# A kernel with three stages on one core: the keys and queries of its random-feature attention split into a high and a low part, copied over all 128 rows by DMA, and multiplied by the feature projection in single-pass products

## The reference

```
x2 = layer_norm(x)                             # twice in a row, merged in the kernel
q, k, v = x2 @ wq + bq, x2 @ wk + bk, x2 @ wv + bv      # 16 heads of width 8
p(t)  = (t @ proj_mat) / sqrt(8)               # "angles": 8 x 128 projection, per token and head
phi(t) = concat(cos(p), sin(p)) / sqrt(128)
kv   = sum over tokens of phi(k)^T v           # per sequence of 256 tokens and head
attn = phi(q) @ kv
y = attn @ wo + bo + residual; y = y + relu(layer_norm(y) @ w1 + b1) @ w2 + b2
```

## Time and profile before

| what | value |
|---|---|
| median of 3 runs | 4777.37 us (4777.08 to 4777.64) |
| the profiled execution, its own time | 4773.44 us |
| span of the profiled execution | 4771.7 us |
| features phase | 0 to about 553 us |
| layers phase | about 554 to 4126 us |
| experts phase | about 4127 us to the end |

### The profile page before, as it was taken

One profiled execution on the slowest core, in us unless ns is written; L12 is line 12 of the kernel. 1 busy time (PEld: TensorE's weight loads), 2 busy tenths in 40 slices (PEclk: granted clock), 3 DMA queues, 4 the chain that ended last, 5 costly groups with the idle time before them and its releaser, 6 DMA issues. The chain is left out here.

```text
span 4771.7 us, 118293 instructions
## 1 busy us (share of the span) xinstructions
PE 4446.4 (93%) x45408; PEld 3473.7 (73%) x45408; DVE 3624.8 (76%) x6437; ACT 3026.3 (63%) x4718; POOL 1787.2 (37%) x966
## 2 busy tenths in 40 slices
PE   6999589999999999999999999999999999689999
PEld 2333278887788877888778887888878888468878
DVE  6888578888788888888878888788888878466553
ACT  5777367676667766776667676766766776233333
POOL 0000155554555545555445554555545555000000
PEclk9999799999999999999999999999999999889999
DMA  0000122222222222222222222222222222100000
GB/s 28 5 5 5 47 62 57 59 56 50 81 58 52 60 65 64 56 60 56 68 61 59 53 59 70 64 53 59 60 70 57 58 60 54 59 7 5 9 7 5
DMA packets 132797, 229.65 MB, mean 48 GB/s; under 512 B 29080, under 2 KB 33824, under 8 KB 131104
## 3 DMA queue, kind: packets, MB, share of 16 engines
q1 hardware_dynamic: 132256, 222.28, 17.9%
HBM read 29.23 MB, written 4.19 MB: 7 GB/s over the span
## 5 line engine op out<-in xcount | busy, mean ns | idle before, releaser
L660 POOL TENSOR_TENSOR qk_rotated<-qk_rotated,rotary_sines 128x1024 f32<-128x1024 f32 x384 | 922.9, 2403 | 1693.3 <-DVE rotary_sines L748 1693.3
L671 POOL TENSOR_TENSOR qk_rotated<-qk_rotated,rnorm 128x1024 f32<-128x1024 f32 x384 | 732.8, 1909 | 7.4
L756 DVE TENSOR_REDUCE qk_sumsq<-qk_squared 128x16 f32<-128x1024 f32 x384 | 467.5, 1218 | 297.6 <-ACT qk_squared L502 297.6
L221 PE MATMUL ps_proj<-qkv_w_hi,x_shifted_hi 128*128 128x512 f32 x1152 | 495.2, 430 | 36.5 <-DVE qkv_w_lo L716 24.0
L509 ACT ACTIVATE q_t<-ps_qk_t 128x512 f32<-128x512 f32 x384 | 229.4, 597 | 464.2 <-PE ps_qk_t L277 464.2
L738 DVE TENSOR_TENSOR qk_rotated<-ps_proj,rotary_scaled 128x1024 f32<-128x1024 f32 x384 | 467.9, 1219 | 7.6 <-ACT qk_squared L502 4.3
L748 DVE TENSOR_TENSOR rotary_sines<-ps_proj,rotary_scaled 128x1024 f32<-128x1024 f32 x384 | 467.0, 1216 | 1.6 <-POOL qk_rotated L660 1.6
L523 ACT ACTIVATE k_t_by_head<-ps_qk_t 64x512 f32<-64x512 f32 x768 | 452.0, 588 | 11.9 <-PE ps_qk_t L286 2.4
L223 PE MATMUL ps_proj<-qkv_w_hi,x_shifted_lo 128*128 128x512 f32 x1152 | 459.1, 399 | 0.0
L222 PE MATMUL ps_proj<-qkv_w_lo,x_shifted_hi 128*128 128x512 f32 x1152 | 458.1, 398 | 0.0
L502 ACT ACTIVATE qk_squared<-ps_proj 128x1024 f32<-128x1024 f32 x384 | 392.2, 1021 | 68.4 <-DVE qk_sumsq L756 50.1
(11 more groups left out here) (248 smaller groups left out, 9723.5 us busy)
## 6 DMA issues: line engine op xcount, KB each, us to landing
v_by_window<-v_tokens SPq DMA_DIRECT2D x1152, 128.0 KB, 2.4
v_by_window<-v_tokens SPq DMA_DIRECT2D x384, 64.0 KB, 2.1
v_by_window<-v_by_window SPq DMA_DIRECT2D x192, 64.0 KB, 2.0
qkv_w_raw<-in_layer_qk_dram SPq DMA_DIRECT2D x7, 1664.0 KB, 7.9
layer_w<-in_layer_w_dram SPq DMA_DIRECT2D x6, 580.5 KB, 3.9
layer_w<-in_layer_w_dram SPq DMA_DIRECT2D x6, 512.0 KB, 3.6
f_x<-in_x_dram SPq DMA_DIRECT2D x8, 256.0 KB, 5.7
x_attn<-f_y SPq DMA_DIRECT2D x8, 256.0 KB, 2.0
```

The lines of the kernel that those rows point to most:

```text
L221: mm(out, hi, HI[:, o:o + 512], start=True, stop=False)
L660: tt(u, u, TB[:], ALU.add).then_inc(added, 1)
L671: tt(u, u, r.unsqueeze(3).broadcast_to((P, 2, 8, DH)), ALU.mult).then_inc(scaled, 1)
L756: nc.vector.reduce_sum(SS[:, 16 * i:16 * i + 16], SQ[:].rearrange("p (h e) -> p h e", e=DH), AX).then_inc(sumsq, 1)
```

## The change

The keys and queries are no longer kept as one float32 tile of which 32 rows are multiplied. ACT writes them, with the bias, into a tile of the single-pass type float32r (the high part: k_hi, q_hi), and a new DVE instruction (k_low at step 11, q_low at step 12) computes PSUM plus bias minus the high part into a low part (k_lo, q_lo). SP then builds, for each of the four groups g of 32 rows, a stacked tile of 128 rows: high, low, high, low. That is 16 DMAs of 32 rows x 512 float32 (64 KB) for the keys and 16 for the queries of each block, SBUF to SBUF. At the start the projection is laid out to match: rows 0 to 63 hold it rounded to float32r, rows 64 to 127 what the rounding left. One float32r product over 128 rows thus sums the four partial products.

Further: project_q moves from step 11 to 12 and project_v from step 13 to 14 on PE, v_out from 13 to 14 on DVE; project_q now waits for the key's high and low part and project_v for the query's, since they overwrite the PSUM bank that those read. The key and query tiles have one buffer each in place of two. k_out waits until the stacked copies of the block before have landed. The store of a block's result is issued two blocks later in SP's list, behind the stacks. The input loads of blocks 1 to 7 share one semaphore.

```diff
-        PB, PBF = sb("proj_blocks", [P, BLK]), sb("proj_scaled", [P, BLK])
+        PB, PST = sb("proj_blocks", [P, BLK]), sb("proj_stacked", [P, BLK], F32R)
...
-        QT, KT = ([sb(f"{x}_t{k}", [P, BLK]) for k in range(2)] for x in ("q", "k"))
+        QHI, QLO, KHI, KLO = (sb(x, [P, BLK], F32R) for x in ("q_hi", "q_lo", "k_hi", "k_lo"))
+        QST, KST = sb("q_stacked", [P, 4, BLK], F32R), sb("k_stacked", [P, 4, BLK], F32R)
...
+        STACK = 16 * 16
...
+            def stack(dst, hi, lo, landed):
+                for g in range(4):
+                    rows = slice(32 * g, 32 * g + 32)
+                    for copy in range(2):
+                        sp.dma_start(dst[64 * copy:64 * copy + 32, g, :].bitcast(F32), hi[rows, :].bitcast(F32)).then_inc(landed, 16)
+                        sp.dma_start(dst[64 * copy + 32:64 * copy + 64, g, :].bitcast(F32), lo[rows, :].bitcast(F32)).then_inc(landed, 16)
+            def stack_k(b):
+                sp.wait_ge(k_hi, b + 1)
+                sp.wait_ge(k_lo, b + 1)
+                if b > 0:
+                    sp.wait_ge(angle, PAIRS * (b - 1) + 8)
+                stack(KST, KHI, KLO, k_in)
+            def stack_q(b):
+                sp.wait_ge(q_hi, b + 1)
+                sp.wait_ge(q_lo, b + 1)
+                after(sp, angle, PAIRS * b)
+                stack(QST, QHI, QLO, q_in)
...
             for i in range(NBLK):
-                sp.wait_ge(xo, 2 * i + 2)
-                sp.dma_start(x_attn[:, i, :], Y[i % 2][:]).then_inc(x_out[i % 2], 16)
+                stack_k(i)
+                stack_q(i)
+                if i > 1:
+                    store(i - 2)
+            store(NBLK - 2)
+            store(NBLK - 1)
...
             def project_q(b):
-                pe.wait_ge(proj_out, 2 * b + 1)
+                pe.wait_ge(k_hi, b + 1)
+                pe.wait_ge(k_lo, b + 1)
...
                 if u == 0:
-                    pe.wait_ge(proj_out, 2 * i + 1)
+                    pe.wait_ge(k_in, STACK * (i + 1))
                 if u == 8:
-                    pe.wait_ge(proj_out, 2 * i + 2)
+                    pe.wait_ge(q_in, STACK * (i + 1))
...
-                        last = mm(out, KT[i % 2][rows, c * P:(c + 1) * P], PBF[rows, :], start=True, stop=True)
+                        last = mm(out, KST[:, r, c * P:(c + 1) * P], PST[:], start=True, stop=True)
...
-                        last = mm(out, PBF[rows, j * P:(j + 1) * P], QT[i % 2][rows, :], start=True, stop=True)
+                        last = mm(out, PST[:, j * P:(j + 1) * P], QST[:, r, :], start=True, stop=True)
...
-                        if u == 11:
+                        if u == 12:
                             project_q(i + 1)
-                        if u == 13:
+                        if u == 14:
                             project_v(i + 1)
...
             def k_out(b):
                 act.wait_ge(proj, 3 * b + 1)
-                a(KT[b % 2][:], NB[:], ACT.Identity, bias=vec(AV_BK)).then_inc(proj_out, 1)
+                after(act, k_in, STACK * b)
+                a(KHI[:], NB[:], ACT.Identity, bias=vec(AV_BK)).then_inc(k_hi, 1)
...
-            ts(PBF[:], PB[:], float(1.0 / (np.sqrt(RD) * 2 * np.pi)), None, ALU.mult).then_inc(setup, 1)
+            ts(PB[:], PB[:], float(1.0 / (np.sqrt(RD) * 2 * np.pi)), None, ALU.mult).then_inc(setup, 1)
+            dve.wait_ge(setup, 4)
+            cp(PST[:], PB[:]).then_inc(setup, 1)
+            dve.wait_ge(setup, 5)
+            tt(PST[64:P, :], PB[64:P, :], PST[64:P, :].bitcast(F32), ALU.subtract).then_inc(setup, 1)
...
+            def k_low(b):
+                dve.wait_ge(k_hi, b + 1)
+                after(dve, k_in, STACK * b)
+                stt(KLO[:], NB[:], vec(AV_BK), KHI[:].bitcast(F32), ALU.add, ALU.subtract).then_inc(k_lo, 1)
...
+                        if u == 11:
+                            k_low(i + 1)
+                        if u == 12:
+                            q_low(i + 1)
-                        if u == 13:
+                        if u == 14:
                             v_out(i + 1)
```

More of the change, by code:

```diff
@@ L963, in features_phase @@
         KV, AB, G, NB = ps("kv"), ps("attn"), ps("tail"), ps("norm")
-        c_in, x_in, x_out, setup = sem("c_in"), [sem(f"x_in{k}") for k in range(NBLK)], [sem(f"x_out{k}") for k in range(2)], sem("setup")
+        c_in, x_in, x_out, setup = sem("c_in"), [sem(f"x_in{k}") for k in range(2)], [sem(f"x_out{k}") for k in range(2)], sem("setup")
         n_mean, n_cent, n_sq, n_var, n_arg, n_bc, n_out, n_aff = (sem("norm_" + x) for x in ("mean", "cent", "sq", "var", "arg", "bc", "out", "aff"))
@@ L968, in features_phase @@
         chain, rn, diag = sem("rs_chain"), sem("rnorm"), sem("diag")
-        proj, proj_out, vpad = sem("proj"), sem("proj_out"), sem("vpad")
+        proj, vpad = sem("proj"), sem("vpad")
+        k_hi, k_lo, q_hi, q_lo, k_in, q_in = (sem(x) for x in ("k_hi", "k_lo", "q_hi", "q_lo", "k_in", "q_in"))
         angle, rounded_act, rounded_dve, frac, fabs, feats, used = (sem(x) for x in ("angle", "rounded_act", "rounded_dve", "frac", "fabs", "feats", "used"))
@@ L973, in features_phase @@
         block = ctx.enter_context(nc.Block())
-        NSETUP = 7
+        NSETUP = 9
+        STACK = 16 * 16
         def vec(k):
@@ L994, in _, with store @@
             for i in range(1, NBLK):
-                sp.dma_start(X[:, i, :], xT[:, i, :]).then_inc(x_in[i], 16)
-            for i in range(NBLK):
-                sp.wait_ge(xo, 2 * i + 2)
-                sp.dma_start(x_attn[:, i, :], Y[i % 2][:]).then_inc(x_out[i % 2], 16)
+                sp.dma_start(X[:, i, :], xT[:, i, :]).then_inc(x_in[1], 16)
+            def stack(dst, hi, lo, landed):
[15 more added lines that the diff above has]
+                stack(QST, QHI, QLO, q_in)
+            def store(q):
+                sp.wait_ge(xo, 2 * q + 2)
+                sp.dma_start(x_attn[:, q, :], Y[q % 2][:]).then_inc(x_out[q % 2], 16)
+            for i in range(NBLK):
+                stack_k(i)
[4 more added lines that the diff above has]
+            store(NBLK - 1)
             for k in range(2):
@@ L1006, in norm_mean @@
             def norm_mean(b):
-                pe.wait_ge(x_in[b], 16)
+                pe.wait_ge(x_in[0], 16) if b == 0 else pe.wait_ge(x_in[1], 16 * (NBLK - 1))
                 if b > 0:
@@ L1050, in angles @@
                 if u == 0:
-                    pe.wait_ge(proj_out, 2 * i + 1)
+                    pe.wait_ge(k_in, STACK * (i + 1))
                 if u == 8:
-                    pe.wait_ge(proj_out, 2 * i + 2)
+                    pe.wait_ge(q_in, STACK * (i + 1))
                 for x in range(2):
                     r = 2 * (u % 2) + x
-                    rows, out = slice(32 * r, 32 * r + 32), TB[U % 2][:, x * BLK:(x + 1) * BLK]
+                    out = TB[U % 2][:, x * BLK:(x + 1) * BLK]
                     if u < 8:
                         c = u // 2
-                        last = mm(out, KT[i % 2][rows, c * P:(c + 1) * P], PBF[rows, :], start=True, stop=True)
+                        last = mm(out, KST[:, r, c * P:(c + 1) * P], PST[:], start=True, stop=True)
                     else:
                         j = u // 2 - 4
-                        last = mm(out, PBF[rows, j * P:(j + 1) * P], QT[i % 2][rows, :], start=True, stop=True)
+                        last = mm(out, PST[:, j * P:(j + 1) * P], QST[:, r, :], start=True, stop=True)
                 last.then_inc(angle, 1)
@@ L1244, in q_out @@
                 act.wait_ge(proj, 3 * b + 2)
-                after(act, angle, PAIRS * (b - 1))
-                a(QT[b % 2][:], NB[:], ACT.Identity, bias=vec(AV_BQ)).then_inc(proj_out, 1)
+                after(act, q_in, STACK * b)
+                a(QHI[:], NB[:], ACT.Identity, bias=vec(AV_BQ)).then_inc(q_hi, 1)
             def k_out(b):
                 act.wait_ge(proj, 3 * b + 1)
-                a(KT[b % 2][:], NB[:], ACT.Identity, bias=vec(AV_BK)).then_inc(proj_out, 1)
+                after(act, k_in, STACK * b)
+                a(KHI[:], NB[:], ACT.Identity, bias=vec(AV_BK)).then_inc(k_hi, 1)
             def kv_scaled(i, s):
@@ L1332, in _ @@
         def _(dve):
-            tt, stt, ts = nc.vector.tensor_tensor, nc.vector.scalar_tensor_tensor, nc.vector.tensor_scalar
+            tt, stt, ts, cp = nc.vector.tensor_tensor, nc.vector.scalar_tensor_tensor, nc.vector.tensor_scalar, nc.vector.tensor_copy
             nc.vector.memset(MEAN[:], 1.0 / D).then_inc(setup, 1)
@@ L1413, in norm_out, with q_low @@
                 tt(XF2(XF, b) if k == 0 else X2N[:], ZC[:], NB[:], ALU.mult).then_inc(n_out, 1)
+            def k_low(b):
+                dve.wait_ge(k_hi, b + 1)
+                after(dve, k_in, STACK * b)
+                stt(KLO[:], NB[:], vec(AV_BK), KHI[:].bitcast(F32), ALU.add, ALU.subtract).then_inc(k_lo, 1)
+            def q_low(b):
+                dve.wait_ge(q_hi, b + 1)
+                after(dve, q_in, STACK * b)
```

(3 more changed lines are left out.)

3 lines of the change are left out of this document (2 added, 1 removed).

## The result

The changed kernel takes 4809.19 us in the median of 4 runs (4807.17 to 4818.46), the kernel before 4777.51 us (4777.08 to 4781.41). By the medians it is slower by 31.7 us. The ratio over all the runs is 1.0075 (95% interval 1.0062 to 1.0088), somewhat more than that of the two medians, 1.0066. The forecast was 4820 us with a range of 4790 to 4856.

A forecast was written before the change was run, and what follows sets the result against it. In the features phase no engine is full; PE, DVE and ACT take turns. 31.5 + 7.6 + 1.2 + 11.2 - 11.2 - 4.5 + 7 = +43 us on 4773.4, plus 4 for timed runs: 4820 us, range 4790 to 4856.

The forecast's parts named there:

- chain at the start: Before the first block's first angle product: the low part and sixteen copies delay it from 38.47 to 46.1, +7.6 us.
- stall a block: At each block change PE, ACT and DVE stand still for the copies: 4.5 us, +31.5 in seven.
- The likeliest case: The forecast itself: late copies stall each block change and outweigh the cheaper products, 4820 us; chance 0.50.
- The angle product: On PE: a pair of single-pass products costs 0.46 us for 1.06 at full clock, 0.6 saved a pair.
- not cheaper here: Rival, angle product: a pair stays near 1 us, the copies' cost remains and the savings go, 4840 us; chance 0.04.
- The chain of copies: From k_out's end to a block's first angle product: low part, sixteen SP issues and landing, 12.5 us where 8.05 were left.
- Cheaper issue: Rival, SP's queue: copies issued every 0.47 us like the loads, not 0.63, about 4792 us; chance 0.18.
- After the stall: PE's work behind the wait, up to tail_out, runs largely at 1.2 GHz: together +1.6 us a block, +11.2.
- The rest of a block: Before use_k and the second norm_rows products save 1.6 us a block; more half-clock stretches cost +1 a block.
- saving of 4.5 us in the first and last block: First block and last pieces of the last: cheaper products count there, -4.5 us (0 to -9).
- The clock stays low: Rival, most of a block: PE at 1.2 GHz, four us a block more, 4848 us; chance 0.20.
- other side: Rival, block changes: the copies fit in the 8.05 us, no one stands still, 4751 us; chance 0.08.

The follow-up runs named there:

- b_nocopies: Changed kernel without the stacking copies, products reading 128 rows of the high part, low parts made but unused: 4761.57 us, ratio 0.9993.
- c_copies_old_products: Changed kernel with low parts, all copies and waits kept, but the old float32 products of 32 rows: 4834.24 us, ratio 1.0126.
- a_split: Changed kernel with PE waiting for the copies in two halves, groups 0 and 1, then 2 and 3: 4784.92 us, ratio 1.0020.
- i_pool_only: Changed kernel with only the copies of groups 2 and 3 issued by GpSimd, PE still waiting for all 16: 4782.26 us, ratio 1.0018.
- f2_after_vback: Changed kernel with only project_v and v_out moved back to step 13: 4809.98 us, ratio 1.0068.
- j_pool_hi_first: Changed kernel with copies shared between SP and GpSimd, waits in two halves, project_v and v_out at step 13, high copies issued first: 4753.14 us, ratio 0.9954.
- h_pool_late_v: Changed kernel with copies shared between SP and GpSimd and waits in two halves, project_v still at step 14: 4780.10 us, ratio 1.0007.

## Why the prediction was right, point by point

| term | forecast us | measured us |
|---|---|---|
| setup | +1.2 | 34.22 - 32.88 = +1.34 |
| chain at the start | +7.6 | (47.34 - 34.22) - (38.47 - 32.88) = +7.53 |
| chain, end of k_out to the first product | 12.5 | 359.66 - 347.20 = 12.46 |
| stall a block | +4.5 | 12.46 - 8.05 = +4.41 |
| the same at the first block change | +4.5 | (103.89 - 91.51) - (91.02 - 84.84) = +6.20 |
| a pair of products, to the start of what follows, full clock | 0.46 | 365.15 - 364.60 = 0.55 |
| first product to attn_out | +1.6 | (371.14 - 359.66) - (464.65 - 453.98) = +0.81 |
| block period in the steady part | 62 to 67.5 | 60.5 to 64.2 |
| features phase | 553 to 596 | 554.5 to 589.5 |
| time | +43 | +31.7 (+35.0 in the profiled phase) |

The likeliest case came about, by its own mechanism. *The angle product* costs nearly what the other phases' rows had said: at full clock the product after a pair starts 0.55 us behind the pair's start (tail_out, L1180, at 365.15), where I had 0.46, and over six blocks a pair saves 0.52 us for my 0.6. The rival "not cheaper here" is out by b_nocopies and c_copies_old_products. *The chain of copies* is exact in each of its terms: 0.79 for the low part, 0.07 to the first issue, 0.63 a copy over fifteen intervals (348.06 to 357.47), 2.2 to the start. All seven later chains are 12.38 to 12.46 us long. "Cheaper issue" is out: the copies go at 0.63 us like those of the earlier trace rows, not at 0.47. The cover of the queries' copies and of the store held: PE waits for none of the first, and after SP's late store, at 370.29, DVE writes its next f_y at 378.86 without having stood.

Two terms were mis-sized on the same side. *After the stall* PE works at half clock for a shorter time than I took:

```profile
359.66:364.00 4.34, 4.34 (x36) 2.04 (x37) 0.00 (x0) 3.00 (x3) 0.00 (x0) 0.62 0.46 105
...
364.00:371.14 7.14, 7.14 (x53) 3.85 (x52) 5.03 (x9) 2.10 (x3) 0.00 (x0) 1.00 0.38 86
```

The granted clock is 0.62 up to 364.00 and 1.00 from there (busy times and clock by stretch, changed kernel). use_q takes 2.98 us for 1.93, project_v and what follows run near full speed, so +0.8 a block and not +1.6, 5.5 us in seven. *The rest of a block* was put at -1.6 + 1 = -0.6. Six blocks take 385.43 us for 362.96: +3.74 a block. Less the stall's 4.41 and the 0.81 that leaves -1.5: 0.9 more saved a block, 6 us in seven. The waits say where: those of ACT for PE at kv_scaled and attn_out have halved. Of the saving of 4.5 us in the first and last block 2.6 came. The first block has 103.89 - 47.34 = 56.55 us for 91.02 - 38.47 = 52.55: +4.0, which is the stall of 6.2 less 2.2. From the last block's first product to the end of the phase it is 589.51 - 489.32 = 100.19 for 100.56, -0.4. That the first block change had only 6.18 us between keys and product I hadn't read in the rows; it adds 1.7. So of the +43 some 11 us were too much and some 3 too little, which makes the 35.0 of the phase; that they partly cancel is luck. "The clock stays low" was a matter of degree: 0.90 after 0.92, not below 0.8.

Two readings of the prediction were wrong and changed little. The 62 us of a block are those of one; six have 60.5 in the mean, so the 67 to 68 foreseen stand against 64.8. And the stretch with a clock of 0.57 was called sparse; PE is busy in all of its 7.60 us.

The *other side*, copies in time and the kernel faster, isn't what comes of copies in time alone. Its figure was 4751, with no one standing still. With the wait halved (a_split), or the issue shared (i_pool_only), the chain was short enough, and still the phase ended 7.0 and 5.2 us later than in the kernel before. The step that I hadn't seen is the move of project_v from step 13 to 14, which the prediction priced only as work behind the stall: it leaves PE with nothing between the third and the fourth hidden row. In the changed kernel the stall covers it (f2_after_vback has the changed kernel's median). Once the copies are in time it shows as a wait of 2.8 us, with the halved clock behind it. With that undone and the high parts copied first, j_pool_hi_first takes 4753.14, near the 4751. The move of project_q from step 11 to 12, which the prediction put at zero, was not undone by itself; what it costs isn't shown.

In h_pool_late_v, after 2.78 us of standing, the granted clock was 0.50, the level of 1.2 GHz; in b_nocopies, after 1.91 us, it was 1.00. The Trainium skill (TensorE: Matmul & The Clock Gate, "Why this matters for your kernels") warns of long idle gaps between bursts of matmuls, after which TensorE falls back to the lower clock. These two rows agree. The Trainium skill says on the same page, in Part 1, that the number of slow matmuls differs from run to run of one kernel. With one trace for each kernel the matmuls can't be counted in two runs; the mean granted clock of h_pool_late_v's ten runs, 0.960 to 0.967, agrees.

## What to carry to other kernels

Count the instructions that a layout change puts in front of a consumer, and multiply by the issue interval of the queue, not by the bytes: sixteen copies of 64 KB were 12.5 us of latency on a path that had 8.05 (6.18 at the first block change), and no engine's busy share shows it. If such a chain is in the way, first start what is ready, let each consumer wait only for its part, and share the issue with an idle queue; then 22 us were won here where 32 had been lost. And where an edit is covered by a stall, price it once more without the stall: it is what remains when the stall is mended.

## What the runs showed of the hardware

- GpSimd issued these 64 KB copies mostly every 0.49 us, SP every 0.63 with GpSimd beside it as without. From the last issue to the start of the reader was 2.2 us with SP alone and 2.86 us with both.
- The time isn't a function of the kernel alone. The runs of b_nocopies lie in two groups some 20 us apart, and the granted clock goes with them: its mean over a run is 0.965 to 0.967 in the six faster and 0.960 to 0.961 in the four slower. That the clock falls after PE's wait for the hidden row, as in h_pool_late_v, is likely and not shown, since only an execution of the faster group was profiled. A place like this is seen in the times of many runs, and one profile can hide it.
